# Attention with decomposed position bias: the bias fill of a tile moved from behind the run of the sums to in front of it

## What is computed

```python
attn = jnp.einsum('bqc,bkc->bqk', q * scale, k)
rel_h = jnp.einsum('bhwc,hkc->bhwk', r_q, Rh)
rel_w = jnp.einsum('bhwc,wkc->bhwk', r_q, Rw)
attn = (attn.reshape(B * nh, h, w, h, w) + rel_h[:, :, :, :, None] + rel_w[:, :, :, None, :]).reshape(B * nh, S, S)
attn = jax.nn.softmax(attn, axis=-1)
out = (attn @ v).reshape(B, nh, h, w, hd)
```

## Time and profile before

| | |
|---|---|
| median of 3 runs | 6808.59 us |
| span of the profiled execution | 6801.4 us |
| TensorE matmul busy | 6725.5 us, 99% |
| VectorE busy | 5454.7 us, 80% |
| ScalarE busy | 4753.7 us, 70% |
| GpSimd busy | 938.1 us, 14% |
| mean granted TensorE clock | 0.996 |

### The profile page before, as it was taken

How to read it: one execution, slowest core, us unless ns; L and a number is a source line. 1 busy time by engine, 2 the same in 40 slices (tenths; PEclk the granted TensorE clock), 3 DMA queues, 4 the chain that set the end, 5 groups by cost and what they waited for, 6 DMA issues and landing times.

```text
span 6801.4 us, 139326 instructions
## 1 busy us (share of the span) xinstructions
PE 6725.5 (99%) x53600; PEld 4245.8 (62%) x53600; DVE 5454.7 (80%) x9973; ACT 4753.7 (70%) x10225; POOL 938.1 (14%) x967
## 2 busy tenths in 40 slices
PE   7999999999999999999999999999999999999998
PEld 5666666666666666666665666666666666666664
DVE  7887888778887788877888778887888878888883
ACT  3776776767767777677776767767676676767775
POOL 2111010211112110121111210102101121101110
PEclk8999999999999999999999999999999999999999
DMA  6676676767677677667676766767677676777673
GB/s 164 148 156 152 137 160 138 163 151 142 152 144 168 144 143 156 149 158 149 142 155 149 158 143 143 161 145 166 140 144 157 147 165 138 143 152 156 144 154 88
DMA packets 306307, 1013.72 MB, mean 149 GB/s; under 512 B 107440, under 2 KB 196976, under 8 KB 215920
## 3 DMA queue, kind: packets, MB, share of 16 engines
q1 hardware_dynamic: 305648, 1004.81, 68.9%
HBM read 745.26 MB, written 255.69 MB: 147 GB/s over the span
## 4 chain that ended last, share of the span: by engine, by line
PE 96%; DMA 1%; DVE 1%; issue 0%; ACT 0%; SPq 0%; POOL 0%; DVEq 0%; ACTq 0%
PE work L805 30%; PE work L878 27%; PE work L796 27%; PE work L824 7%; PE work L843 3%; PE work L862 2%; PE work L851 1%; DMA moving<-rel_scratch 1%; DVE mpart L683 1%; PE work L830 0%; DVE xb L674 0%; ACT probs L561 0%; DMA back<-attention_scratch 0%; DVE hi L721 0%; PE work L835 0%
## 5 line engine op out<-in xcount | busy, mean ns | idle before, releaser
L683 DVE TENSOR_REDUCE mpart<-work 128x1 f32<-128x512 f32 (+1 forms) x8640 | 5088.7, 632 | 1079.7 <-PE work L805 1013.1
L561 ACT ACTIVATE probs<-work 128x512 f32<-128x512 f32 (+1 forms) x8640 | 4100.2, 564 | 866.6 <-PE work L796 852.1
L805 PE MATMUL work<-mkeys,hi 128*128 128x512 f32 (+1 forms) x8640 | 3404.1, 395 | 10.6 <-DVE mpart L683 8.8
L796 PE MATMUL work<-moving,keys 113*128 113x512 f32 (+1 forms) x8640 | 3299.9, 383 | 10.9 <-DMA moving<-rel_scratch 5.7
L805 PEld LDWEIGHTS work<-mkeys,hi 128*128 128x128 f32 x8640 | 1643.6, 190 | 622.4 <-DVE mpart L683 324.0
L878 PE MATMUL work<-probs,vall 128*17 128x288 f32 x27648 | 2013.1, 409 | 0.0
L796 PEld LDWEIGHTS work<-moving,keys 113*128 113x128 f32 x8640 | 1642.1, 190 | 362.3 <-ACT probs L561 39.2
L878 PEld LDWEIGHTS work<-probs,vall 128*17 128x17 f32 x27648 | 637.3, 96 | 846.8 <-ACT probs L561 358.3
L824 PEld LDWEIGHTS work<-image,tab 128*48 128x48 f32 x6912 | 401.6, 124 | 544.9 <-ACT probs L561 513.2
L490 POOL TENSOR_TENSOR full<-full,hi 128x384 f32<-128x384 f32 x576 | 583.5, 1016 | 938.7 <-DVE hi L721 937.6
L495 POOL TENSOR_TENSOR rden<-oraw,rden 128x576 f32<-128x576 f32 x96 | 137.1, 1428 | 3955.3 <-DMA rden<-inverse_scratch 3955.3
(11 more groups left out here) (42 smaller groups left out, 646.8 us busy)
## 6 DMA issues: line engine op xcount, KB each, us to landing
moving<-rel_scratch SPq DMA_DIRECT2D x1728, 144.0 KB
moving<-qk_scratch SPq DMA_DIRECT2D x288, 576.0 KB
rel_scratch<-hi SPq DMA_DIRECT2D x192, 432.0 KB, 5.7
rel_scratch<-full SPq DMA_DIRECT2D x192, 432.0 KB, 5.5
moving<-rel_scratch SPq DMA_DIRECT2D x288, 288.0 KB
image<-qk_scratch SPq DMA_DIRECT2D x384, 144.0 KB, 3.2
keys<-qk_scratch SPq DMA_DIRECT2D x192, 288.0 KB, 7.8
qk_scratch<-split_hi SPq DMA_DIRECT2D x144, 192.0 KB, 3.9
```

What stands on the lines that cost most here:

```text
L561: act.activation(probs[:, tile % RING, lo:up], bank[:, 0:up - lo], ACT.Exp).then_inc(act_read, 1)
L683: dve.tensor_reduce(mpart[:, u % 2, q, m:m + 1], bank[:, 0:MSPLIT[m][1] - MSPLIT[m][0]], AX.X, ALU.max)\
L796: pe.matmul(bank[:, 0:up - lo], tile_of(keys[0:K_ROWS, u % 2, :], c, third), moving[0:K_ROWS, slot_of(u, third)[0], lo:up], start=True, st ...
L805: pe.matmul(bank[:, 0:up - lo], hi[:, u % 2, q * P:(q + 1) * P], mkeys[:, u % 2, lo:up], start=True, stop=True).then_inc(for_dve, 1)
```

## The change

The bias fill is put at i = 5 (`SB`) of its tile, and TensorE does the items of the plan at i = 5 before the sums. ScalarE's code already walks the plan to i = 5, and the numbers of the banks follow the plan.

```diff
             if t < 12 and u + 2 < UNITS:
-                plan[u][t][0].insert(0, ("rel", u + 2, t))
+                plan[u][t][SB].append(("rel", u + 2, t))
...
                     for i in range(SB + 1):
+                        for item in plan[u][t][i]:
+                            fill(item)
                         if i == SB and 0 < tile <= TILES * UNITS:
                             attend(tile - 1)
-                        for item in plan[u][t][i]:
-                            fill(item)
                         if 0 <= u < UNITS and i < SB:
                             fill(("score", tile, i))
```

## The result

The changed kernel takes **6973.74 us** (median of 5 runs, 6973.04 to 6977.6) against 6811.73 us for the kernel before (5 runs, 6806.47 to 6817.65, the three known beforehand among them): a ratio of **1.0238, 95% interval 1.0226 to 1.0251**, 162 us slower. The profiled executions differ by 6975.8 - 6801.4 = 174 us in span; the one of the changed kernel was the longest of its five, the one of the kernel before the shortest of its own.

The account below looks back on a forecast made before the run. TensorE was taken as the bound, busy 99% of the span. Plain tiles 39 + 43, tile 1 40 and qk tiles 46 gave 168 us on 6808.6, so 6977 us, range 6900 to 7060.

Parts of the forecast that it names:

- What the fill waits for: Before the sums in a plain tile: fill's load waits for ScalarE's read of score block 2, 0.18 us after block 4.
- From the fill to the sums: TensorE's fill loads 0.18 or 0.36 us, last matmul 0.04 or 0.02, then a gap taken as 0.10 before the sums.
- Plain tiles: Tiles without special work: +0.10 us in 394 with four matmuls (39 us), +0.09 in 473 with eight (43 us).
- Tile 1: Tile 1 of a unit, copies of old sums delay block 2's read: +0.61 us in 65 tiles, 40 us.
- Tiles with qk: Tiles with a qk fill, where the bias fill waits for the qk read: 126 tiles at 0.365 us, 46 us.
- Tiles with statistics: 70 tiles where TensorE already waits 0.20 us for VectorE: no loss taken, 7 us if that cover were gone.
- The sum: All tile kinds together: 39 + 43 + 40 + 46 = 168 us more, giving 6977 us, 2.5% slower.
- The range: Total time from 6900 to 7060 us, meant to leave out no more than 2 in 10.
- second rival: Also rival 2: gap from fill to sums is 0.22 us, not 0.10; 127 us more, 7104 us; chance 8%.
- The rest: ScalarE's copy, VectorE's rounding, SyncE's load and the stores don't move the end; clock stays at its upper level.
- signs named beforehand: Fill loads idle until the exponential or qk read; plain tiles 3.69 and 3.85, tile 1 4.30, qk 5.24; TensorE below 99%.
- two rules weighed: On TensorE: weight loads pulled ahead, plain tiles costing about nothing; a tiling-mode change drains the engine, speaking for more cost.

Follow-up runs that it names:

- experiments 5 and 6: On experiment 2 and experiment 1 respectively, ScalarE's exponential of score block 2 cut to 64 of 512 columns in plain tiles: 6804.85 and 6809.13 us.
- experiment 5: On experiment 2, fill in front of the sums, ScalarE's exponential of score block 2 cut to 64 of 512 columns in plain tiles: 6804.85 us, ratio 0.9996.
- experiment 2: Against the changed kernel, fill put behind the sums in tile 1 of a unit and qk tiles, still in front elsewhere: 6885.89 us, ratio 1.0113.
- experiment 3: Against the changed kernel, fill in front of the sums only in tile 1 of a unit and qk tiles, behind them elsewhere: 6897.65 us, ratio 1.0129.
- experiment 1: Against the changed kernel, TensorE does the sums first and the fill behind them, the plan kept at i = 5: 6805.82 us, ratio 0.9998.
- experiment 8: Against the changed kernel, the fill moved to i = 3, in front of block 3: 6938.99 us, ratio 1.0195.
- experiment 4: Against the changed kernel, the fill moved one block earlier, in front of block 4: 6953.2 us, ratio 1.0211.

## Why the prediction was right

The forecast was 6977 us, the measurement 6974 us. Over the five runs of the kernel before that is 162 us instead of 168, over the 6808.6 us that the forecast started from 165.

- **What the fill waits for.** Right: the fill's load starts 0.05 after the read of score block 2 and 0.19 after score block 4 (0.18 said). Shown by experiments 5 and 6: they shorten nothing but that read, and with it goes the whole cost of the plain tiles.
- **From the fill to the sums.** Right: sums 0.50 after score block 4 (0.50 said), and the gap of 0.10 that no row showed measured 0.09 in experiment 5.
- **Plain tiles.** With four matmuls 3.69 - 3.58 = 0.11 (0.10 said), x 394 = 43 us. With eight the single tiles of the two tables give 3.84 - 3.77 = 0.07, but that pair is untypical: the medians over all plain tiles of the kind are 3.85 and 3.76, 0.09 as said, and whole tiles added up give 40 us. Together 83 us against 82 said, and 76 in the medians or 81 in the span of experiment 2. Two typical tiles with eight, of experiment 2 (in front) and of experiment 3 (behind):

```profile
2555.28:2559.13 3.85, 3.85 (x36) 2.56 (x35) 3.18 (x6) 2.82 (x6) 0.20 (x1) 1.00 1.09 210
2559.68:2563.44 3.76, 3.76 (x36) 2.48 (x35) 3.18 (x6) 2.83 (x7) 0.00 (x0) 1.00 1.11 184
```

- **Tile 1.** 4.30 - 3.69 = 0.61 as said, x 65 = 40 us. In its timeline below (ScalarE's block 2, then TensorE) the load goes 0.79 and the sums 1.11 after score block 4, both as said.
- **Tiles with qk.** 5.24 - 4.87 = 0.37 and 5.42 - 5.03 = 0.39 (0.37 and 0.36 said), 63 of each; all 126 added up give 47 us, 46 said.
- **Tiles with statistics.** In tile 3 nothing, 3.78 against 3.79, as said; the tiles with statistics other than tile 1 lose under 2 us together. Not covered are the seven that are tile 1 too: 4.30 against 3.78, 7 x 0.52 = 4 us that I had at nothing. A cover of 0.20 hides a stall of 0.10 but not one of 0.61.
- **The sum** of these tiles is 43 + 40 + 40 + 47 + 4 = 174 us, against 173 between the spans of the changed kernel and of experiment 1 (6975.8 - 6803.0) and 168 said: the forecast was some 5 us low on the profile, mostly by those seven tiles. The medians differ by 162. That forecast and median meet within 3 us is partly luck, since runs of one kernel spread by more than that (6801 to 6818 us for the kernel before).
- **The range.** Its upper end, 7060, is called half of the second rival, but half of its 127 us gives 7041.
- **The rest.** Experiment 1 shows that the later copy, rounding and stores cost nothing. The granted clock is 1.00 in every stretch shown.

That tile 1:

```profile
2564.90 0.63 ACT L561 ACTIVATE probs<-work 128x512 f32<-128x512 f32 x1
...
2564.79 0.38 PE L796 MATMUL work<-moving,keys 113*128 113x256 f32 x1
2565.58 0.39 PE L824 MATMUL work<-image,tab 128*48 128x96 f32 x4 [0.41 <-ACT probs L561]
2565.90 0.44 PE L878 MATMUL work<-probs,vall 128*17 128x288 f32 x4
```

Of the signs named beforehand, two were weak. TensorE's busy share only fell from 98.9 to 98.1%, for the reason given at the first fence. And idle time of the fill's weight loads, ended by the exponential, tells nothing by itself: the kernel before has it as well, while the sums run (0.48 each in the earlier trace rows), 513 us in all against 271 in the changed kernel. What tells is the same wait ended by the qk read, of which the kernel before has none (85 us now), and when the load starts: 0.05 after the read.

Of the two rules weighed, the one from the Trainium skill, *TensorE: Matmul & The Clock Gate*, section "Step-by-step: what each phase is for", that weight loads are pulled ahead of running matmuls, holds where nothing is waited for: in experiment 5 the load starts together with score block 4. It doesn't hold past a wait on the load itself, and that is this change. The other, also of the Trainium skill, *TensorEngine Tiling (Array Packing)*, section "Key Properties", says that a change of tiling mode drains the engine; the 0.09 to 0.10 us in front of the sums agree with it. It doesn't say that weights of 48 columns are a mode of their own, so it did not by itself speak for rival 2, and in experiment 5 they add no drain of their own.

## What to carry to other kernels

With n banks in turn, the work that stands in front of fill k decides whether the read of fill k - n is in time. A long run that needs no bank (here 1.09 us of sums) is the place where the reader catches up, and a fill belongs behind it, not in front: moving it in front turned the run's cover into a wait in nearly every tile with a fill. To price such a move, count back n fills, take the end of that read from the timeline, and work with distances between starts, since the busy time of matmuls swallows stalls of 0.1 us.

## What was not expected

- A narrow fill between wide ones costs more than behind the sums even when no bank is waited for: 3.83 against 3.77 us with eight matmuls (experiment 8); by the reading of experiment 4, because the next wide weight load lies bare. The cheap place for narrow matmuls is beside the sums: behind them, and in front of them too where no read is waited for (experiments 5 and 6).
- A wide matmul whose weight load is let go late delays what follows by more than its start shows: the sums come 0.31 to 0.32 us after that load (experiments 4 and 8, and tile 1 before).
- Of 174 us more in span, 121 appear in the profile as more TensorE busy time with the same instructions.
